# A convolution, attention and feed-forward kernel: cross products no longer joined, attention values weighted in four column groups

## The reference, cut to what matters

```python
x = x + conv(group_norm(x), kernels)       # 11 x 11 depthwise, padding 5; kernels = 96x4 weights @ 4 cones
t = to_tokens(x)                           # (16, 256, 96)
qkv = layer_norm(t) @ w_attn               # 6 heads of 16
q, k = rope(q), rope(k)
wei = softmax(causal(q @ k.T * 0.25))      # (16, 6, 256, 256)
t = t + (wei @ v) @ w_proj
t = t + ffn(layer_norm(t))                 # 96 -> 384 -> 96, sign weights, activations clipped by group maxima
```

## Time and profile before

| what | value |
|---|---|
| median of three runs | 279.45 us (278.80 to 280.39) |
| the profiled execution, and its span | 276.62 us, 274.7 us |
| TensorE matmul busy | 227.3 us, 83% |
| TensorE weight loads busy | 169.4 us, 62% |
| VectorE busy | 202.3 us, 74% |
| ScalarE busy | 136.8 us, 50% |
| GpSimd busy | 112.6 us, 41% |
| granted TensorE clock, mean | 0.928 |

### The profile page before, as it was taken

One profiled execution on the slowest core, in us unless ns is written; L12 is line 12 of the kernel. 1 busy time (PEld: TensorE's weight loads), 2 busy tenths in 40 slices (PEclk: granted clock), 3 DMA queues, 4 the chain that ended last, 5 costly groups with the idle time before them and its releaser, 6 DMA issues.

```text
span 274.7 us, 5248 instructions
## 1 busy us (share of the span) xinstructions
PE 227.3 (83%) x1718; PEld 169.4 (62%) x1718; DVE 202.3 (74%) x514; ACT 136.8 (50%) x308; POOL 112.6 (41%) x143
## 2 busy tenths in 40 slices
PE   6487497988785976979899988969999779999990
PEld 5467486977665864656576766747775525555550
DVE  3858539999994558954788877867565968988966
ACT  1421316766570446336578756847684616145260
POOL 1201125745652344347448654395636453110102
PEclk9659989999996899566999999999999999999998
DMA  4941522787796869001445443000000000101103
GB/s 125 253 158 51 170 67 70 139 150 126 147 138 125 138 123 95 4 0 45 106 100 101 89 90 89 2 3 0 4 2 0 1 2 0 43 2 44 43 0 100
DMA packets 27548, 20.25 MB, mean 74 GB/s; under 512 B 3969, under 2 KB 26882, under 8 KB 27522
## 3 DMA queue, kind: packets, MB, share of 16 engines
q1 hardware_dynamic: 25920, 18.64, 33.3%
q10 hardware_dynamic: 1602, 1.29, 2.0%
HBM read 6.03 MB, written 1.57 MB: 28 GB/s over the span
## 4 chain that ended last, share of the span: by engine, by line
PE 46%; DVE 11%; SPq 9%; issue 7%; ACT 3%; DMA 2%; POOL 1%; DVEq 0%; POOLq 0%; ACTq 0%
PE bank L1778 7%; PE bank L1659 7%; SPq L435 6%; PE bank L1602 5%; PE bank L1539 5%; DVE nmax L1105 4%; SPq L402 3%; PE bank L1570 3%; PE bank L1461 3%; PE bank L1605 2%; DMA pt_ring<-xs_ring 2%; PE bank L1450 2%; PE bank L1551 2%; PE bank L1643 1%; PE bank L1627 1%
## 5 line engine op out<-in xcount | busy, mean ns | idle before, releaser
L1105 DVE TENSOR_REDUCE nmax<-bank 128x3 f32<-128x384 f32 x64 | 45.4, 751 | 18.8 <-PE bank L1539 18.7
L762 ACT ACTIVATE pt_ring<-bank 128x384 f32<-128x384 f32 x96 | 42.0, 491 | 13.7 <-PE bank L1572 12.9
L560 POOL TENSOR_SCALAR_AFFINE_SELECT pt_ring<-pt_ring 128x512 f32<-128x512 f32 x48 | 30.9, 648 | 36.1 <-ACT pt_ring L762 36.1
L517 POOL TENSOR_TENSOR parts<-rest_ring,parts 96x512 bf16<-96x512 f32 x16 | 20.8, 1299 | 30.1 <-ACT parts L694 30.1
L1439 PE MATMUL bank<-xs_ring,toep 128*128 128x192 f32 x144 | 29.3, 352 | 1.2 <-DVE xs_ring L971 1.2
L1439 PEld LDWEIGHTS bank<-xs_ring,toep 128*128 128x128 f32 x144 | 26.4, 208 | 2.8 <-issue 2.1
L1539 PE MATMUL bank<-stack 128*128 128x128 bf16 (+1 forms) x288 | 24.4, 233 | 4.2 <-DVE nmax L1105 2.4
L1539 PEld LDWEIGHTS bank<-stack 128*128 128x128 bf16 (+1 forms) x288 | 19.1, 105 | 10.2 <-issue 7.0
L1570 PE MATMUL bank<-stack 97*128 97x256 bf16 x96 | 23.9, 284 | 0.5 <-ACT pt_ring L762 0.5
L1778 PE MATMUL bank<-parts,w_b 128*96 128x512 f32 (+1 forms) x60 | 23.1, 492 | 1.5 <-issue 1.3
L1659 PE MATMUL bank<-parts,w_b 97*128 97x256 f32 (+1 forms) x60 | 23.2, 500 | 0.0
(11 more groups left out here) (151 smaller groups left out, 489.0 us busy)
## 6 DMA issues: line engine op xcount, KB each, us to landing
stack<-parts SPq DMA_DIRECT2D x96, 96.0 KB, 3.6
stack<-in_const SPq DMA_DIRECT2D x9, 192.0 KB, 3.3
pt_ring<-xs_ring SPq DMA_DIRECT2D x14, 120.0 KB, 3.3
tok<-in_x_tok SPq DMA_DIRECT2D x4, 384.0 KB, 7.6
out<-xs_ring SPq DMA_DIRECT2D x4, 288.0 KB, 2.6
stack<-in_x ACTq DMA_DIRECT2D x2, 384.0 KB, 8.5
stack<-nmax_t SPq DMA_DIRECT2D x32, 1.5 KB
pt_ring<-xs_ring SPq DMA_DIRECT2D x14, 36.0 KB, 2.6
```

What stands on the lines that cost most here:

```text
L517: nc.gpsimd.tensor_tensor(part(b, 2), rest_ring[:, u], part(b, 1), ALU.subtract).then_inc(s_p2, 1)
L560: nc.gpsimd.affine_select(out=v, in_=v, compare_op=ALU.is_ge, fill=0.0, base=0, pattern=[[0, 2], [0, 2], [1, P]], channel_multiplier=-1).t ...
L762: nc.scalar.activation(pt_ring[:, b % 2, h, :], bank[:, 3 + h % 2, 0:T + P], ACT.Exp, scale=float(HD) ** -0.5).then_inc(s_exp, 1)
L1105: last = nc.vector.tensor_reduce(nmax[:, b % 2, k:k + 3], bank[:, 0:3, first:first + (t + 1) * P], op=ALU.max, axis=AX.X, negate=True)
```

## The change

There are three edits. Cross products are no longer joined: `convolve` runs all four points in each part, `join_toep`, `join_xs`, `toep_join`, `xs_join` and their semaphores go, and with them the 48 transfers that SyncE issued for them. The constant rows are loaded by two transfers, slots 0 to 5 ahead of the first stack and slots 6 to 8 between the stacks of images 5 and 6. And the values are weighted in four column groups: heads 0 to 3 on partitions 0 to 127, with heads 4 and 5 in a third block of 128 columns, split by query tile over the four groups; `o_ring` becomes 128 x 384, the four transposes of 96 rows become three of 128 rows, and the division becomes two instructions.

```diff
-JOINED = [(0, 2, 0, REACH, 0, 0), (3, 1, 0, P - REACH, REACH, 0), (3, 1, P - REACH, REACH, REACH, 1)]
...
+PV_ORDER = ([(h, h, 0, P, T, 0) for h in range(4)] + [(h, h, 1, 0, P, P) for h in range(4)]
+            + [(0, 4, 0, T, P, 2 * P), (1, 5, 0, T, P, 2 * P), (2, 4, 0, P, P, 2 * P), (3, 5, 0, P, P, 2 * P)]
+            + [(0, 4, 1, 0, P, 2 * P), (1, 5, 1, 0, P, 2 * P)])
...
-        o_ring = sb("o_ring", [C, 2, 2 * T])
+        o_ring = sb("o_ring", [P, 2, 3 * P])
...
-            sp.wait_ge(s_toep, POINTS)
-            for t in range(NT):
-                join_toep(t)
-            join_xs(1)
             for k in range(2, 4):
                 load_tokens(k)
             sp.dma_start(wp[:], w_proj).then_inc(s_weights, 16)
...
+            def causal(first, last):
+
+                words = stack[KROWS:P, first:last, :, :, :].rearrange("p r h s n -> p (r h) (s n)").bitcast(F32)
+                table = const[KROWS:P, N_CONST:N_TABLE].unsqueeze(1)
+                sp.dma_start(words, table.broadcast_to([P - KROWS, HEADS * (last - first), T])).then_inc(s_causal[first > 0], 16)
...
-            for j in range(2, PAIRS):
-                join_xs(j)
-                for slot in range(2 * (j - 2), min(2 * (j - 1), RING)):
-                    causal(slot)
-                for b in (2 * j - 7, 2 * j - 6):
-                    if b >= 0:
-                        stack_image(b)
+            causal(0, 6)
+            for b in range(6):
+                stack_image(b)
+            sp.wait_ge(s_xn, PAIRS)
+            causal(6, RING)
+            for b in range(6, RING):
+                stack_image(b)
             max_row(0)
             max_row(1)
...
-                nc.scalar.copy(o_ring[:, b % 2, :], bank[0:C, 7, :]).then_inc(s_o, 1)
+                nc.scalar.copy(o_ring[:, b % 2, :], bank[:, 7, 0:3 * P]).then_inc(s_o, 1)
...
-                for p in (0, 1, 3, 2):
+                for p in range(POINTS):
...
-                    if p in (1, 3):
-                        last.then_inc(s_xsp, 1)
...
-                nc.vector.tensor_tensor(o_norm[:].rearrange("p t (h d) -> p (t h) d", d=HD), o[:, :, 0:HD],
-                                        rsum[:].unsqueeze(2).broadcast_to([P, NT * HEADS, HD]),
-                                        ALU.mult).then_inc(s_on, 1)
+                heads = o_norm[:].rearrange("p t (h d) -> p t h d", d=HD)
+                for blocks, to in ((slice(0, 8), heads[:, :, 0:4, :]), (slice(8, 12), heads[:, ::-1, 4:HEADS, :])):
+                    by = rsum[:, blocks].rearrange("p (t h) -> p t h", t=NT).unsqueeze(3)
+                    last = nc.vector.tensor_tensor(to, o[:, blocks, 0:HD].rearrange("p (t h) d -> p t h d", t=NT),
+                                                   by.broadcast_to([P, NT, to.shape[2], HD]), ALU.mult)
+                last.then_inc(s_on, 1)
...
-                if part == 1 and n0 >= 1:
...
-                    pe.wait_ge(s_toepj, 16 * 2 * len(JOINED))
-                    pe.wait_ge(s_join[t][s], 16 * len(JOINED) * ((n0 + 1) // 2))
-                    for q, rows in ((0, P), (1, 2 * REACH - P + REACH)):
...
+                    if b == 6:
+                        pe.wait_ge(s_causal[1], 16)
...
-                for g in range(2):
-                    for t in range(NT):
-                        for e in range(3):
...
+                for row, h, keys, first, n, to in PV_ORDER:
+                    rows = slice(2 * HD * row, 2 * HD * (row + 1))
+                    begins = keys == 0
+                    ends = keys == 1 or to == 2 * P and row >= 2
+                    last = nc.tensor.matmul(bank[rows, 7, to:to + n], v_ring[:, s, keys, h, :],
+                                            pt_ring[:, s, h, first:first + n], start=begins, stop=ends)
...
-                for t in range(NT):
-                    for g in range(2):
-                        k = 2 * t + g
-                        last = nc.tensor.transpose(bank[:, 5, k * C:(k + 1) * C],
-                                                   o_ring[:, b % 2, g * T + t * P:g * T + (t + 1) * P], ident[0:C, 0:C])
+                for k in range(3):
+                    last = nc.tensor.transpose(bank[:, 5, k * P:(k + 1) * P], o_ring[:, b % 2, k * P:(k + 1) * P], ident[:])
...
-            pe.wait_ge(s_causal, 16 * RING)
+            pe.wait_ge(s_causal[0], 16)
```

More of the change, by code:

```diff
@@ L246, in build @@
         s_grid = sem("s_grid")
-        s_causal = sem("s_causal")
+        s_causal = [sem(f"s_causal{i}") for i in range(2)]
         s_qzero = sem("s_qzero")
@@ L250, in build @@
         s_toep = sem("s_toep")
-        s_toepj = sem("s_toepj")
-        s_xsp = sem("s_xsp")
-        s_join = [[sem(f"s_join{t}{s}") for s in range(2)] for t in range(NT)]
         s_gst = sem("s_gst")
```

38 lines of the change are left out of this document (removed).

## The result

The changed kernel takes 262.32 us (median of 4 runs, 259.80 to 264.81), the kernel before 279.12 us in the same job (4 runs, 278.71 to 280.39). The ratio is 0.936, with a 95% interval of 0.929 to 0.944. The profiled execution took 262.38 us, with a span of 260.5 us.

What follows compares the result with a forecast made beforehand. SyncE's transfer list, 13.0 us a round, was slower than the engines' 9.62 us step. Removing joins (10.3 us) and four column groups (2.8 us) give 13.1 us off 276.62, 263.5 us, or 266.3 us from the median; range 261 to 272 us.

Steps and rivals of the forecast that it cites:

- Pairs 5, 6 and 7: Convolution steps without TensorE's waits on joined transfers: 0.67, 6.10 (with the low clock behind the wait) and 1.8 us gained.
- Pair 1: Convolution start without the 2.49 us wait on joined transfers: 1.7 us gained, bounds 1.7 and 3.6.
- the lower case: Pair 1's gain if the low clock recurs between the group norm's two sums: 1.7 us.
- Extra products: Two more products a convolution step, 0.65 us, hidden in TensorE's 1.02 us wait: nothing; 4.6 us if that cover is gone.
- SyncE and the constant rows: SyncE's round falls to 12 transfers, 7.8 us; the two constant-row transfers cost nothing, bounds 0 and +2 us.
- Rival 5: Long constant-row transfers hold SyncE or the transfer engines, stacks are late; half of part 1 remains, 271.5 us; chance 0.04.
- The stages' meeting: From 109.40 to 128.20 us, where the stages meet, the forecast kept the low clock, near 0.6 for 15 us or more.
- rival 1: The clock holds where the stages meet: 4.5 us more gained, 261.8 us; chance 0.22.
- Part 3: Weighted values in four column groups: 0.21 us less an image, 2.8 us in all after the division, bounds 0 and 3.2.
- rivals 3 and 4: Weighted values: fourth column group costs what it saves, 269.5 us, chance 0.07; or groups run one behind another, 305 us, 0.03.

Runs made afterwards that it cites:

- with 18: Kernel before with the constant rows in two transfers instead of nine, joined products and their copies kept; 281.27 us, ratio 1.012.
- the other execution: Profiled execution of the unchanged changed kernel, run once more in another job; it took 267.38 us, the median there 264.31 us, ratio 0.943.
- the meeting filled: Changed kernel with unread identity products in three idle gaps of TensorE, plus eight more where the stages meet; 261.76 us, ratio 0.941.
- The kernel with thirteen more of them: Kernel with eleven unread products in pair 1's idle time, plus six before image 9's weighted values and seven before the last image's; 260.83 us, ratio 0.940.

## Why the prediction was right, point by point

The forecast, 266.3 us, is 4.0 us above the median measured, inside its range, and its main reasons held. The gain forecast was 13.1 us. Between the profiled executions it was 276.62 - 262.38 = 14.24 us, 1.1 us more; between the medians it was 16.8 us, 3.7 us more. The terms below account for the first. The 2.6 us between the two are not traced to any row: before's profiled execution lay 2.5 us under its median, the changed kernel's on its own, and two executions of one kernel differ by more than that (262.38 and 267.38 us). Term by term, in the first execution:

- **Pairs 5, 6 and 7**: forecast 0.67, 6.10 and 1.8, measured 0.68, 6.09 and 1.71 us. Right. The reason, a list of transfers slower than the engines, is shown by the kernel that keeps the joined form and loses the waits by order alone. My sum of the round, 20 transfers of 0.65 us to issue, was only half of it: with 18 pair 6's copies came sooner as the sum says, but pair 7's landed late behind a large transfer. The forecast did not rest on 18, but its view that time to issue decides was too simple.
- **Pair 1**: forecast 1.7 us, bounds 1.7 and 3.6, measured 3.71 us. This is the term that was mis-sized. I took the case with the low clock; in the profiled execution the clock held. In the other execution it fell for some 10 us, pair 2's convolution started at 38.37 us and the term was nothing, below my lower bound: I had priced a low clock of the length seen before, and it can last longer. So the sum was helped by a term that is decided anew in each execution. (By its own figures the lower case is 2.4 - 0.65 = 1.8 us.)
- **Extra products**: forecast nothing. Right for pairs 2 to 6: 0.45 us more in a step of the same length, and still one product of room. Not for pair 7, whose step has no such wait: 0.3 us there.
- **SyncE and the constant rows**: forecast nothing. Right: no wait on them is left. The first landed in 18.6 us, the second in 5.9 us, for my 20 and 10. Rival 5 didn't come about; what it describes, a long transfer that holds up the ones behind it, shows in the kernel with two transfers of constant rows and the copies kept.
- **The stages' meeting**: I forecast the low clock as before, rival 1 that it holds. In the first execution rival 1's condition came about for the most part: the clock is 1.00 from 93.99 to 110 us and 0.81 in the last 6 us, where it had a mean of 0.59 over 18.8 us. Its price did not: 2.0 us, not 4.5. TensorE was busy for 16.04 of 18.80 us, 85%; now, from 93.99 to 113.99 us, for 9.00 + 4.68 of 20.00 us, 68%. What it no longer spends at the low clock it mostly waits, for VectorE's maxima and ScalarE's exponentials. In the second execution the forecast's condition came about, a low clock for 13.6 us, and the gain there was 22.01 - 21.48 = 0.5 us. So the change doesn't settle what the clock does there, and the clock is worth 1.5 us. That the time came out near rival 1's (261.8 us) is luck: it got there by another sum.
- **Part 3**: forecast 0.21 us an image and 2.8 us in all. Measured 0.17 to 0.24 us an image in runs of steps at the full clock; 1.65 us by image 9 and 0.78 us from image 10 to 15, 2.4 us, against before, and 2.9 us over all images against the kernel with the old form and parts 1 and 2. Weighted values 1.21 us for 1.43, transposes 0.33 as before, division 0.42 us for two instructions. Right. Four column groups ran side by side, and rivals 3 and 4 are refuted. The trace goes on disagreeing with the Trainium skill ("TensorE: Matmul & The Clock Gate", "Part 3: Packing small matmuls", The mechanism): it says that loads overlap running matmuls only where the row groups differ. All 28 instructions use all 128 rows, so by that sentence no load should overlap. Yet in the profile the loads are busy for 0.9 us an image (14.6 us over 16 images) and the matmuls for 1.28 us, while on the chain the whole takes 1.21 us.
- **Not foreseen**: in the first execution the clock fell at image 9 and at the last image, 1.2 and 1.0 us lost, behind idle stretches as long as before's (1.47 and 1.71 us), where it had held. In the second it held at image 9. That the change brought these falls is not shown.

## What to carry to other kernels

When a queue that computes nothing has a share of the chain, write down the order of its list and what stands ahead of each transfer that an engine waits for; reordering may give most of what removing them gives. Count the bytes ahead of it, too, and not only the transfers. Before an addition is costed at nothing, read the wait that is to hide it in every step that it enters, and test it by a dose: in four steps one more product was free here and a second was not, and in the step without that wait none was. Take a gain worked out from one profiled execution off that execution's time, and quote the distance to the median apart. And profile a kernel twice before a stretch at the low clock is put down to a change.

## What the runs showed of the hardware

- The clock granted to TensorE need not be the same in two executions of one kernel at the same place: after the same idle 2.65 us it held in one and stood at 0.50 for some 10 us in the other, 4.2 us apart; where the stages meet it was low for 3.4 us in the one and 13.6 us in the other. The means over the span, 0.950 and 0.945, don't show it; windows of 2 us do.
- A fall can wipe out what a held clock gained: with the meeting filled, image 0's values came 1.2 us sooner and image 2's 1.6 us later, behind a fall of some 7 us from 118 us on. What brought that fall stays open, since the same idle stretches had none behind them in four other executions.
- Useless products in idle time delayed nothing that the profiles show (the sums of pair 1 start 4.48 us behind the transposes of pair 2, and 4.47 us without them). The kernel with thirteen more of them was 2.4 us faster in its profile, which a clock that held by chance would explain as well.
- One transfer of 1152 KB took 0.43 us to issue; one of 192 KB took 0.44 to 0.77 us. It landed in 18.6 us behind the opening loads and in 11.1 us where it was issued at 29.4 us. The 1728 KB by two transfers in place of nine gained nothing by itself (281.27 against 279.65 us).
- Copies of 24 to 120 KB landed in 1.9 to 3.5 us before, and in 6.2 to 6.7 us when issued 4.8 us behind a transfer of 576 KB and the stacks after it.
